# Top-2 expert FFN on routed tokens in blocks of 512 instead of all four experts on every token

## The reference, cut to what matters

```python
scores = jnp.einsum('bsd,de->bse', x, gate_w) + gate_b
probs = jax.nn.softmax(scores, axis=-1)
topk_vals, topk_idx = jax.lax.top_k(probs, TOP_K)              # TOP_K = 2
mask = jnp.sum(jax.nn.one_hot(topk_idx, NUM_EXPERTS, dtype=probs.dtype), axis=-2)
masked = probs * mask
masked = masked / (jnp.sum(masked, axis=-1, keepdims=True) + 1e-09)
h = jax.nn.gelu(jnp.einsum('bsd,edh->ebsh', x, w1) + b1[:, None, None, :], approximate=False)
y = jnp.einsum('ebsh,ehd->ebsd', h, w2) + b2[:, None, None, :]
out = jnp.einsum('bse,ebsd->bsd', masked, y)
...
x = x + _L0_conv_ref(_gn(x), ...)
t = _to_tokens(x)
t = t + _L1_attn_ref(_ln_t(t), ...)
t = t + _L1_ffn_ref(_ln_t(t), ...)
```

## Time and profile before

| | us |
|---|---|
| median of 3 runs | 4033.3 (4031.06 to 4038.34) |
| span of the profiled execution (the page gives no time outside it) | 4009.3 |
| PE busy in it | 3540.4 |
| DVE busy | 2293.3 |
| ACT busy | 1733.3 |
| POOL busy | 144.9 |
| mean granted clock of TensorE | 0.932 of full speed |

### The profile page before, as it was taken

The page is one execution under the profiler, slowest core; times in us unless marked ns, Lnnn a source line. Parts: engine busy times, 40 slices in busy tenths (PEclk is TensorE's granted clock), DMA queues, the critical chain, the costliest instruction groups (busy, mean ns, idle before and its releaser), DMA issues.

```text
span 4009.3 us, 68583 instructions
## 1 busy us (share of the span) xinstructions
PE 3540.4 (88%) x24347; PEld 2432.0 (61%) x24347; DVE 2293.3 (57%) x6031; ACT 1733.3 (43%) x4063; POOL 144.9 (4%) x132
## 2 busy tenths in 40 slices
PE   0698989999899899989989998999989989998998
PEld 0466665666666566666656666566666656666665
DVE  3445655656656465655646466564665646565554
ACT  0132634536253363625436263452625336362542
POOL 0000000000000000000000000000000000000000
PEclk9569989999999899999999899998999989999989
DMA  3100000000000000000000000000000000000000
GB/s 48 46 13 4 13 8 13 7 3 14 8 13 8 13 6 4 14 8 14 8 13 6 3 13 8 13 7 2 14 8 13 8 13 6 4 14 8 5 5 9
DMA packets 68306, 44.26 MB, mean 11 GB/s; under 512 B 58909, under 2 KB 59970, under 8 KB 66372
## 3 DMA queue, kind: packets, MB, share of 16 engines
q10 hardware_dynamic: 8416, 30.67, 2.5%
q1 hardware_dynamic: 59492, 8.53, 1.7%
HBM read 21.07 MB, written 12.84 MB: 8 GB/s over the span
## 4 chain that ended last, share of the span: by engine, by line
issue 60%; PE 25%; DVE 8%; POOL 2%; ACT 2%; SPq 0%; DMA 0%; ACTq 0%; POOLq 0%; DVEq 0%
PE PSUM L1137 3%; PE PSUM L1213 2%; PE PSUM L1310 2%; PE PSUM L1134 1%; PE PSUM L1217 1%; PE PSUM L1215 1%; ACT HF L583 1%; PE PSUM L1194 1%; PE PSUM L1195 1%; PE PSUM L1196 1%; PE PSUM L1197 1%; PE PSUM L1198 1%; PE PSUM L1174 1%; DVE X L840 1%; PE PSUM L1230 1%
## 5 line engine op out<-in xcount | busy, mean ns | idle before, releaser
L583 ACT ACTIVATE HF<-PSUM,B 128x512 f32<-128x512 f32 x768 | 509.1, 685 | 732.3 <-PE PSUM L1198 672.0
L1213 PE MATMUL PSUM<-W2H,HHI 128*128 128x192 f16 x3072 | 770.2, 251 | 23.0 <-DVE HLO L828 23.0
L1217 PE MATMUL PSUM<-W2H,HLO 128*128 128x192 f16 x3072 | 765.1, 249 | 0.0
L1215 PE MATMUL PSUM<-W2L,HHI 128*128 128x192 f16 x3072 | 764.8, 249 | 0.0
L825 DVE TENSOR_SCALAR HHI<-HF 128x512 f16<-128x512 f32 x768 | 323.3, 421 | 673.4 <-ACT HF L583 672.5
L828 DVE SCALAR_TENSOR_TENSOR HLO<-HF,HHI 128x512 f16<-128x512 f32 x768 | 531.6, 692 | 26.4
L622 ACT ACTIVATE PS<-PSUM,NMX 94x126 f32<-94x126 f32 x1056 | 366.0, 357 | 114.6 <-DVE NMX L867 77.7
L1213 PEld LDWEIGHTS PSUM<-W2H,HHI 128*128 128x128 f16 x3072 | 313.1, 102 | 132.9 <-issue 41.9
L1230 PE MATMUL PSUM<-KBD,QT 96*94 96x378 f32 x704 | 312.6, 528 | 41.3 <-issue 39.7
L1215 PEld LDWEIGHTS PSUM<-W2L,HHI 128*128 128x128 f16 x3072 | 303.9, 99 | 40.2 <-issue 14.1
L867 DVE TENSOR_REDUCE NMX<-PSUM 94x3 f32<-94x378 f32 x352 | 188.4, 544 | 231.9 <-PE PSUM L1233 207.2
(11 more groups left out here) (233 smaller groups left out, 5542.4 us busy)
## 6 DMA issues: line engine op xcount, KB each, us to landing
XR<-in_x ACTq DMA_DIRECT2D x16, 768.0 KB, 5.6
out_dram<-X ACTq DMA_DIRECT2D x32, 384.0 KB, 2.3
GUP<-TGU SPq DMA_DIRECT2D x256, 8.0 KB, 1.8
TGU<-HSP SPq DMA_DIRECT2D x128, 8.0 KB, 1.8
XG<-HSP SPq DMA_DIRECT2D x128, 8.0 KB, 1.8
HF<-in_w ACTq DMA_DIRECT2D x3, 384.0 KB, 3.3
X<-in_w ACTq DMA_DIRECT2D x3, 384.0 KB, 3.2
XG<-XN SPq DMA_DIRECT2D x16, 64.0 KB, 2.3
```

The lines of the kernel that those rows point to most:

```text
L583: act.activation(HF[:, n % 2, :], PSUM[:, 4 + n % 2, :], ACT.Gelu, scale=1 / (X_UP * W_UP), bias=B1[:, ek:ek + 1]).then_inc(s["gelu_done"], 1)
L1213: pe.matmul(dst, HHI[:, n % 2, tok], W2H[:, e * HK + k, :], start=False, stop=False, skip_group_check=True)
L1215: pe.matmul(dst, HHI[:, n % 2, tok], W2L[:, e * HK + k, :], start=False, stop=False, skip_group_check=True)
L1217: mm = pe.matmul(dst, HLO[:, n % 2, tok], W2H[:, e * HK + k, :], start=False, stop=(k == HK - 1), skip_group_check=True)
```

## The change

The kernel now sorts tokens by expert. Each expert owns a region of the DRAM tensor slots, in which its tokens of all images follow each other. A row has 800 bytes: the normalised token as high and low f16 parts, its four gates and its number. In attention(i):

- at b=0 DVE computes the gates of all 8 tiles of image i-1; at b=2 PE counts winners (prefix), DVE turns this into slot numbers (positions) and picks the full blocks of 512 rows to be worked on (schedule, SCHED);
- POOL writes the rows to slots with 16 indirect DMAs of 128 rows (scatter), two for each tile;
- SP then loads for each block the expert's weights (WB, 1.6 MB from a DRAM copy, double-buffered), the block's tokens by a transposing DMA (XT) and its gates and numbers (META).

No FFN chunk runs in attention. experts(i) runs 4 blocks (image 1: one, image 0: none) of 6 chunks; a block's result is multiplied by its gate on DVE (Y) and added into out by 4 indirect accumulating DMAs on POOL (add). X2 itself is stored to out by ACT beforehand. At the end (i = B) 10 blocks are run, the partly filled ones among them, with cleared region ends. So 67 blocks, 402 chunks, take the place of 768. The router works in f32 on turned tokens (XNT), without split parts. The setup clears WB, splits weights in 20 pieces and stores them to DRAM.

The core of the diff:

```diff
+BS = 512
+NSEL = 4
+NSEL_END = 10
+XRING = 4
+CAP = B * T + BS
+SLOT_ROW = 400
+WROW = 6400
+W_A, W_2H, W_2L, W_B2, W_B1 = 0, 3840, 4992, 6144, 6336
+LINKS_0, LINKS_1, LINKS = 72, 67, 73
...
+            def tokens(i, j):
+                if j >= NSEL:
+                    sp.wait_ge(f["ffn1_done"], upto("ffn1_done", i, j - XRING, HK))
+                    sp.wait_ge(f["added"], upto("added", i, j - XRING, 16 * 4))
+                row = sp.value_load(SCHED[0:1, j, 0:1], min_val=0, max_val=E * CAP - BS)
+                k = xslot(i, j)
+                sp.dma_start_transpose(XT[:, k, :, :], slots[bass.ds(row, BS), 0:2 * C]).then_inc(x_loaded[k], 16)
+                sp.dma_start(METAI[:, k, :, 0:5],
+                             slots[bass.ds(row, BS), 2 * C:2 * C + 10].bitcast(I32).rearrange("(q p) c -> p q c", p=128)
+                             ).then_inc(x_loaded[k], 16)
+            def expert(i, j):
+                if j >= 2:
+                    sp.wait_ge(f["ffn2_chunk"], upto("ffn2_chunk", i, j - 2, HK))
+                sp.sem_inc(w_chosen, 1)
+                row = sp.value_load(SCHED[0:1, j, 1:2], min_val=0, max_val=(E - 1) * 128)
+                k = wslot(i, j)
+                sp.dma_start(WB[:, k, :].bitcast(I32), weights[bass.ds(row, 128), :]).then_inc(w_loaded[k], 16)
+            def selected(i):
+                if second(i):
+                    sp.wait_ge(weights_stored, 16 * E)
+                sp.wait_ge(s["scattered"], at("scattered", i, 0))
+                sp.wait_ge(s["sched_ready"], at("sched_ready", i, 0))
+                if isinstance(i, int) and i == B:
+                    sp.wait_ge(ends_cleared, 16 * E)
+                for j in range(min(blocks_of(i), 2)):
+                    expert(i, j)
+                for j in range(min(blocks_of(i), XRING)):
...
+                state_moves(i + 1)
+                expert(i, 2)
+                expert(i, 3)
+            selected(B - 1)
+            expert(B - 1, 2)
+            expert(B - 1, 3)
+            clear_ends()
+            selected(B)
+            for j in range(2, NSEL_END):
+                expert(B, j)
+                if j + 2 >= XRING and j + 2 < NSEL_END:
+                    tokens(B, j + 2)
...
+            def scatter(i):
+                if not second(i):
+                    pool.wait_ge(f["added"], upto("added", i, 0))
+                pool.wait_ge(s["slots_ready"], at("slots_ready", i, 0))
+                pool.sem_inc(moves_begun, 1)
+                for k in range(2):
+                    for t in range(NT):
+                        pool.indirect_dma_start(
+                            slots[:, :].bitcast(I32), bass.IndirectOffsetOnAxis(IDX[:, k, t:t + 1], 0),
+                            XROW[:, t, :].bitcast(I32), None,
+                            bounds_check=E * CAP - 1, oob_is_err=False).then_inc(s["scattered"], 16)
...
+            def add(i, j, last_blocks=False):
+                for half in range(2):
+                    pool.wait_ge(s[X2_FREE[half]], at(X2_FREE[half], i, 1))
+                if not second(i):
+                    pool.wait_ge(f["added"], upto("added", i, j))
+                pool.wait_ge(f["y_ready"], upto("y_ready", i, j, 1))
+                pool.sem_inc(moves_begun, 1)
+                for q in range(4):
+                    row = TOKT[:, j % 2, q:q + 1] if last_blocks else METAI[:, xslot(i, j), q, E:E + 1]
+                    pool.indirect_dma_start(
+                        out[:, :], bass.IndirectOffsetOnAxis(row, 0), Y[:, wslot(i, j), q, :], None,
+                        bounds_check=B * T + BS - 1, oob_is_err=True, compute_op=ALU.add).then_inc(f["added"], 16)
...
+            def image(i):
+                if not first(i):
+                    scatter(i)
+                if not last(i):
                     rstd(i + 1, GR[:], GV[:], 2, "gn_eps", "gn_rstd")
                 token_rstd(i, 1)
                 token_rstd(i, 0)
-                if following:
-                    conv(i + 1)
+                if not last(i):
+                    conv_states(i + 1)
+                if not first(i):
+                    add(i, 0)
+                if not last(i):
+                    conv_tokens(i + 1)
+                if not first(i):
+                    for j in range(1, blocks_of(i)):
+                        add(i, j)
             rstd(0, GR[:], GV[:], 2, "gn_eps", "gn_rstd")
-            conv(0)
+            conv_states(0)
+            conv_tokens(0)
             image(0)
-            with pool.Fori(1, B - 1) as i:
+            image(1)
+            with pool.Fori(2, B - 1) as i:
                 image(i)
-            image(B - 1, following=False)
+            image(B - 1)
+            scatter(B)
+            for j in range(NSEL_END):
+                add(B, j, last_blocks=True)
         @block.scalar
...
             def store(i, half):
-                act.wait_ge(s["ffn_added"], at("ffn_added", i, E * (2 - half)))
+                act.wait_ge(s["x2_ready"], at("x2_ready", i, 4 - 2 * half))
...
+                rows = out[bass.ds(i * T, T), :].rearrange("(p t) c -> p t c", t=NT)
+                act.dma_start(rows[:, tiles, :], X2[:, tiles, :]).then_inc(s[X2_FREE[half]], 16)
...
+            def block_out(i, j):
+                dve.wait_ge(f["ffn2_chunk"], upto("ffn2_chunk", i, j, HK))
+                if j >= 2:
+                    dve.wait_ge(f["added"], upto("added", i, j - 2, 16 * 4))
+                ws = wslot(i, j)
+                dve.tensor_tensor(Y[:, ws, :, :].rearrange("p (a b) c -> p a b c", a=2),
+                                  PSUM[:, 6:8, 0:2 * C].rearrange("p a (b c) -> p a b c", b=2),
+                                  YG[:, ws, :].rearrange("p (a b) -> p a b", a=2).unsqueeze(3).broadcast_to(
+                                      (128, 2, 2, C)), ALU.mult).then_inc(f["y_ready"], 1)
...
@@ -869,26 +1060,21 @@
                                               AX.X, ALU.max, negate=True).then_inc(s["max_done"], 1)
                     if following and b == 3:
                         norm_variance(i + 1)
-                    if before and b >= 4 and b % 3 == 1:
-                        add_expert(i - 1, E + (b - 4) // 3)
                     if b >= 1:
                         copy_turned(2 * b - 2)
-                        if before:
-                            split(i - 1, half0 + 2 * b - 2)
                         copy_turned(2 * b - 1)
-                        if before:
-                            split(i - 1, half0 + 2 * b - 1)
                         normalize(b - 1)
                     if before and b == 0:
-                        gates(i - 1, 0)
+                        gates(i)
+                    if before and b == 2:
+                        positions(i)
+                        schedule(i)
                     if following and b == 1:
                         norm_channels(i + 1)
                     if following and b == 4:
...
+            def positions(i):
+                dve.wait_ge(s["prefix_done"], at("prefix_done", i, 0))
+                fill = FILL[:].unsqueeze(1).broadcast_to((128, NT, E))
+                link(dve.tensor_tensor(SLOT[:], PSUM[:, 4, 0:NT * E].rearrange("p (t e) -> p t e", e=E), fill, ALU.add))
+                dve.tensor_tensor(FILL[:], FILL[:], PSUM[:, 4, NT * E:(NT + 1) * E], ALU.add)
+                link(dve.scalar_tensor_tensor(SLOT[:], SLOT[:], 1.0, WINB[:], ALU.add, ALU.mult))
+                dve.tensor_reduce(SMAX[:], SLOT[:], AX.X, ALU.max)
+                dve.tensor_copy(ROWTOK, TOKF[:])
+                link(dve.tensor_reduce(SSUM[:], SLOT[:], AX.X, ALU.add))
+                dve.tensor_scalar(IDX[:, 0, :], SMAX[:], -1.0, None, ALU.add)
+                dve.tensor_scalar(TOKF[:], TOKF[:], float(T), None, ALU.add)
+                dve.scalar_tensor_tensor(IDX[:, 1, :], SSUM[:], -1.0, SMAX[:], ALU.add, ALU.subtract
+                                         ).then_inc(s["slots_ready"], 1)
...
+            def schedule(i, last_blocks=False):
...
+            link(dve.memset(WB[:], 0.0))
             for n, _ in enumerate(conv(0)):
-                if n % 3 == 0 and n // 3 < len(WEIGHTS):
-                    split_weights(n // 3)
-            attention(0, False, True)
...
+            attention(0)
+            finish((rest(0), conv(1)))
+            assert links[0] == LINKS_0, links[0]
+            links_from(LINKS_0)
+            attention(1)
+            experts(1, rest(1), conv(2))
...
-            links_from(LINKS_FIRST + (B - 2) * LINKS)
-            attention(B - 1, True, False)
-            experts(B - 1, 1, rest(B - 1))
-            gates(B - 1, 0)
-            experts(B - 1, 0)
+            links_from(LINKS_0 + LINKS_1 + (B - 3) * LINKS)
+            attention(B - 1)
+            experts(B - 1, rest(B - 1))
+            gates(B)
+            positions(B)
+            schedule(B, last_blocks=True)
...
+            def ffn1(i, j, k):
+                xs, ws = xslot(i, j), wslot(i, j)
+                if k == 0:
```

(97 more changed lines are left out.)

536 lines of the change are left out of this document (290 added, 246 removed).

## The result

The changed kernel takes 4115.3 us (median of 4 runs, 4110.8 to 4124.0), the one before beside it 4032.2 (4015.8 to 4038.3): a ratio of 1.0226, 95% interval 1.0187 to 1.0265. It is slower by 2.3%, though it computes 402 chunks in place of 768. Two later repeats, on two chips, gave 1.0272 (1.0214 to 1.0331) and 1.0263 (1.0199 to 1.0328).

A forecast was written before the change was run, and what follows sets the result against it. TensorE, busy 88% of the span, was taken as the bound. Terms +6 - 16 + 0 - 27 - 62 - 11 + 165 = +55 gave span 4064, plus 24 outside it: 4088 us, 1.4% slower; 8-in-10 range 3955 to 4235.

The forecast's parts named there:

- Attention is dear without FFN because of the clock: Attention loop: without FFN chunks TensorE gets 1.2 GHz, and a round costs 6.40 us against 4.09 at 2.4 GHz.
- clock stays up in attention: Rival, chance 0.06: attention keeps the high clock, 20.7 us less 3 for a longer scatter wait, times 15: 3823 us.
- X, POOL's price of a scatter: POOL's time per indirect DMA in attention, taken as 1.4 us; the wait for GR is 16X - 16.3, so 6.
- cheap scatter: Rival, chance 0.22: an indirect DMA costs POOL 0.64 us, so no wait in attention: 3989 us, faster by 1.1%.
- The two readings of the clock: Attention's clock: the skill's rule, read as busy time, promises the high clock; the trace held busy f32 matmuls at 0.50.
- Attention, 97.5 + 6 = 103.5: Attention of a steady image: image 0's 89.0 us plus DVE's additions and an earlier clock fall, then 6 of wait.
- headroom of 3 us for PE: Attention's wait for GR: PE has about 3 us queued, half a round, when DVE starts to wait.
- a wait of XG put down to GR: Sign to look for in attention: the wait before XG on DVE is put down to GR.
- Experts, 128.5: Expert stage of a steady image: 128.5 us instead of 130.4, with the clock back within the first rounds.
- The tail, 236: After the last image: 62 us in series, 10 blocks at 16.6, then 8 for the last accumulates; 236, so +165.
- The case of slow reads: Rival, chance 0.10: transposed reads and loads take 15 us each, delaying tail, state_moves and experts 1: 4310 us.
- The setup, +6: Setup: WB's memset, 20 pieces for 14 in splitting weights, and XROW together add 6 us.

The follow-up runs named there:

- fill8: The changed kernel with 8 idle f16 matmuls more in every attention round of images 2 to 15: 3925.4 us, 0.9764 of the kernel before.
- fill4: The changed kernel with 4 idle f16 matmuls a round of attention, GR still behind the scatters: 3916.4 us, 0.9786 of the kernel before.
- after_third: The changed kernel itself, unchanged, run again on the third chip: 4114.0 us, 1.0263 of the kernel before.
- no_rows0: The changed kernel without the two DVE operations that make the rows of tiles 0 to 3: 4048.4 us, 1.0067 of the kernel before.
- gr_first: The changed kernel with GR ahead of the 16 scatters on POOL: 3975.7 us, 0.9881 of the kernel before; again on the third chip 4118.5, 1.0269.
- fill4_gr: The changed kernel with 4 idle matmuls a round of attention and GR ahead of the scatters: 3970.1 us, 0.9884; again on the third chip 3918.9, 0.9803.

## Why the prediction came out as it did

The direction and the time within 27 us (4088 against 4115) were right, and the range held it. But by its own sign the forecast as a whole was wrong: a steady image takes 238.9 us, over the 238 that it named. That the time came near is in part luck: the expert stages cost 97 us more than forecast, and a cheaper tail, a cheaper setup and an added 24 us where 1.8 lie hid most of it. Step by step:

- **Attention is dear without FFN because of the clock**: right, shown by fill8 and fill4. The case "clock stays up in attention" was not what the change does, but its price, 17.7 us an attention, was near what the idle matmuls gave: 102.8 to 85.9 on average on one chip (after_third, fill4).
- **X, POOL's price of a scatter**: taken 1.4, measured 1.28. The case "cheap scatter" decided at 1.0 and fell. POOL was held for 1.28 us by each scatter, and 16 more of them put 20.4 us on the path. The Trainium skill, "DMA: Bandwidth & Descriptors", section "Anatomy of one DMA — SWDGE (gpsimd) path", says that writing descriptors costs little; the trace does not agree.
- **The two readings of the clock**: the granted clock rose from 0.51 to 0.85 when 4 f16 matmuls were added in each round (fill4), and stood at 0.50 with the f32 ones alone at 98.8% busy. The Trainium skill, "TensorE: Matmul & The Clock Gate", section "What's actually happening", says that matmul activity releases the throttle: with the f16 matmuls added the trace agrees, with the f32 ones alone it does not.
- **Attention, 97.5 + 6 = 103.5**: 102.9 on average, by two errors that cancel. Without any wait it is 93.3 (gates, positions and the earlier fall of the clock cost 4 over image 0's 89.3, not 8.5), and the scatters cost 7 to 10, not 6. The terms of the sum, 89.0 + 2.5 + 3 + 3 - 1.3, give 96.2; 97.5 leaves the -1.3 out, and with it the forecast would be some 20 us lower. The wait's mis-sized part was the headroom of 3 us for PE: by the formula 1.28 gives 4.2, while in no_rows0 DVE waited 8.1 and PE still 7.1. The sign of it, a wait of XG put down to GR, showed on the first chip alone; in the trace of the changed kernel the same time went by in waits released by "remote".
- **Experts, 128.5**: this step failed. They take 136.0 on average, 7.5 x 13 = 97 us more than forecast, and 5.5 more than before (130.5), where I had expected 1.9 less. PE is busy for 118.1 us of a stage in place of 114.6, and idle for 2.1 more. Two terms stood at nothing. The f32 router's 16 matmuls take 1.85 us where the 20 f16 ones of before took 0.65 (rows of PE, start and duration; before in the first fence, after in the second), two times a stage, so 2.4 us:

```profile
782.59 0.18 PE L1330 MATMUL PSUM<-GWAH,XH 128*128 128x4 f16 x1 [2.28 <-DVE XL L936]
...
783.08 0.16 PE L1334 MATMUL PSUM<-GWB,XL 128*128 128x4 f16 x1
```

```profile
1486.59 1.85 PE L1570 MATMUL PSUM<-GATEW,PSPT 96*128 96x4 f32 x16
```

  And the clock: 20.5 us of the stage at 1.2 GHz, 16.4 before, a mean over images 2 to 14 from the clock records, so 4.1 us more at half speed, at most 2 of time. I had read the recovery as quick. That makes at most 4.4 of the 7.5, argued from rows: no run changed the router alone. Another 1.9 is the saving that I had forecast and that nothing shows. The rest stays open; the making of the rows is not it (no_rows0).
- **The tail, 236**: 209.7, with three terms off. The first block began 47 us after the last chunk's end (3903.1), not 62: weights and the transposed read landed in 13 us, not 27. The case of slow reads fell with this. Blocks run at 14.87 us (bias matmuls of blocks 2 and 10 start at 3969.8 and 4088.8, over 8), not 16.6. My 16.6 was no block at full clock. The three steps in the kernel before were these, columns as in rows 2:

```profile
3942.90:3960.40 17.50, 16.45 (x107) 9.67 (x107) 7.83 (x17) 4.12 (x6) 0.00 (x0) 0.83 0.00 1
3960.40:3977.10 16.70, 15.65 (x107) 9.66 (x107) 7.96 (x17) 4.12 (x6) 0.00 (x0) 0.90 0.00 0
3977.10:3992.20 15.10, 13.90 (x107) 8.69 (x107) 7.88 (x17) 4.12 (x6) 0.00 (x0) 1.00 0.00 1
```

  At a clock of 1.00 a block took 15.1 already then, so all that changed between the two, the missing additions into X2 among it, is worth 0.3. (The four starts also lie 1.6 us apart in the last expert, not 1, so the mean of the three is 16.4.) From the last matmul to the end it took 14.9, not 8: an accumulate costs 1.86 where I had 1.4, the first starts 2 us after the matmul, and the last ends on POOL 5.8 before the span does. The line of the bias matmuls in the new tail, columns as in rows 3:

```profile
L1456 PE MATMUL PSUM<-WB,ONES x40: 251/252/336, 3954.6 to 4090.4; 3*128 3x192 bf16 x40
```

  The timeline of PE at the first block's start (its wait in brackets):

```profile
3950.24 3.17 PE L1441 MATMUL PSUM<-XT,WB 128*128 128x512 f16 x7 [43.16 <-DMA META<-slots]
```

  The last accumulate on POOL:

```profile
4109.32 1.56 POOL L674 DMA_INDIRECT out_dram<-Y,TOKT  x1 [0.30 <-issue]
```

- **The setup, +6**: attention 0 starts at 213.7 where it started at 215.4: -1.7, so WB's memset and the further splits cost nothing that can be seen. Attention 15: 95.5, not 91.6. Experts 1: 111.8, not 115.
- **The 24 us outside the span**: wrong as a step. The profiled execution after took 4118.5 us with a span of 4116.7, so 1.8 lie outside. The 24 were the difference between a fast profiled execution of before and its median; its expert stages vary from 125 to 142 us with the clock. In spans the change is +107 us, in medians +83, and the forecast was +55 for both.

Sum of the steps against the span of 4064: experts +97, tail -26, setup -8, attention 15 +4, attention and experts 1 -7, images' attention -7: 4117, the measured 4116.7.

## What to carry to other kernels

Work that runs in the gaps of another stage and keeps the clock up can cost far less than the time that it takes alone. Before removing it, look for a stretch of the same trace without it and take the difference (89.0 against 103.9, so 15 us for 24 chunks), not its own time (four blocks at 15.1, so 60 us). If it must go, put back a few idle matmuls and measure. When a price is read from a stretch, read the clock of that stretch with it: the 16.6 of a block was 15.1 at full clock. And compare variants on one chip only: here one and the same kernel, gr_first, was 1.2% faster than the kernel before on one chip and 2.7% slower on another, while the median of every kernel with idle matmuls lay below that of the kernel before.

## What the runs showed of the hardware that I had not expected

- f32 matmuls that keep PE 98.8% busy were granted 0.50; 4 f16 matmuls of 128x512 among them in each round lifted the clock of attention 5 to 0.85 (fill4), 8 to 0.88 (fill8), and the 4 saved 17 of 103 us on average (after_third, fill4).
- While POOL issues its 16 scatters, other engines stand in waits that end on no known engine's event, the longest 14.8 us (ACT, fill4_gr), in nine traces, and in none of the four from the first chip. During the accumulates of the same traces there are none.
- In these traces an indirect DMA of 128 rows holds POOL for 1.28 us when it writes 800 bytes a row without arithmetic, 1.86 us when it accumulates 768 bytes a row.
- A transposing read of 512 rows of 384 f16 landed in 3.8 us (median of 67, the changed kernel).
